# Keys spread from digits by TensorE, quartered loads, earlier zeroing and a stored one-hot in a four-layer graph network

## The chip, the cores and the metric

The kernel is one launch on one core of a Trainium2 chip. The metric is the device time of the launch in microseconds. Before the change it was 3574.64 us, the median of 3 runs (3573.5 to 3580.78 us). All times below are microseconds (us) unless marked ns.

## The reference

A graph of 3125 nodes with 32 features each and 100000 edges (`src`, `dst`, sorted by `dst`; `dst = int(3125 * u**2)`, so low numbers have many edges; `src` is uniform). Four layers, each `x = x + layer(relu(layernorm(x)))`:

```python
# layer 0: sum of edge attributes per source node, then a small network
agg = segment_sum(edge_attr_32, src); h = relu([x, agg] @ W1.T + b1)
out = batchnorm(h) @ W2.T + b2
# layer 1: a message per edge, summed per destination node
R = relu(w[:, None] @ w1 + b1) @ w2 + b2          # radial weights, 384 per edge
msg = tensor_product(R, directions(edge_attr_3), features[src])
out = zeros.at[dst].add(msg)                      # 32 values per edge
# layer 2: three rounds of out = clip(0.9 * A_w @ out + 0.1 * y, 0, 1), normalised weights
# layer 3: three rounds of z = batchnorm(relu(A_c @ z)), normalised counts and self-loops
```

`A_w` holds the summed weights and `A_c` the number of edges of each (source, destination) pair.

## The kernel before, in words

Nodes are padded to `NP` = 3200 (25 tiles of 128), edges to 100352, that is `CH` = 784 chunks of 128, one edge per partition. The host lays edge `784*p + c` at partition p of chunk c. A step is 4 chunks; there are `STEPS` = 196.

The matrices of layers 2 and 3 are built in DRAM in `both`, 3200 x 3200 pairs (count, weight), 82 MB. GpSimd first writes zeros there (41 DMAs, L543 and L547), and then adds one chunk after another with an indirect DMA that accumulates (`add`, L557): 128 rows of 8 bytes, at row `key = 3200*src + dst`. `add(c)` waits until `add(c-2)` has landed, so two are in flight. Edges of one chunk or of neighbouring chunks with the same key must be merged before: for that every key is compared with every other one of the group.

**First stage** (layer 0, and the merging of chunks 0 to 391): two steps make a group of 4 merged chunks. SyncE loads the group's 512 keys from `keys_dram`, broadcast to all 128 partitions (`load_keys`, L405, 256 KB), and per 4 steps 16 chunks of edge attributes (`load_attr`, L417, 256 KB). ScalarE squares the differences of keys (`compare_group`, L614) and turns them into a 0/1 matrix (L619). VectorE masks it (L1201), TensorE counts with small matmuls (L850 to L864), VectorE writes the entries and their places (L1209 to L1214). Besides, each step sums 4 chunks of attributes by source node: one-hots of the low part of the node number (ScalarE L639, L644; VectorE L1264) as weights, and as moving data the attributes times a one-hot of the high part (`prod0`, L1273, from the stored one-hot `high0` made at L1182), in 20 matmuls (`scatter0`, L879). All buffers are double.

**Between the stages** the small network of layer 0 runs, and the node table is written to `feat_dram` (L436). The constant tiles that all engines wait for (`s_const`) are made by GpSimd ahead of the zeroing.

**Second stage** (layer 1, and the merging of chunks 392 to 783): per step GpSimd gathers 4 chunks of node rows (`gather`, L565) and issues 2 adds, in program order after all adds of the first stage; TensorE does the merging matmuls, 8 matmuls for the radial weights of the next step (L949) and 20 for the sum by destination (`scatter`, L888); VectorE makes the messages (L1384 to L1422) and four products (`products`, L1242), each the message times the test `iota_a == a_dst` of the high part, computed on the spot. Chunk k of `scatter` waits for product k alone.

**Third stage**: layers 2 and 3 read `both` (L1472 on), 50 loads and then matrix products. It starts when all adds have landed.

Of the kernel before, what the change touches and what calls it, by code (L numbers as in the profile page):

```python
# [31 lines left out]
STEPS = CH // 4  # L32
PAIRS = CH // 2
# [52 lines left out]
def gnn_program(nc, x_in, src_in, dst_in, srcT_in, dstT_in, ea3_in, ea32_in, ew_in, ewT_in,  # L86
                w1T_in, b1_in, gamma_in, beta_in, w2T_in, b2_in, l1w1_in, l1b1_in, l1w2_in, l1b2_in,
                gam3_in, bet3_in, out):
    with ExitStack() as ctx:
# [9 lines left out]
        keys_dram = nc.dram_tensor("keys_dram", [CH, P], F32, kind="Internal").ap()  # L99
        feat_dram = nc.dram_tensor("feat_dram", [NP, ROW], F32, kind="Internal").ap()  # L100
# [20 lines left out]
        zc = sb("zc", [P, FEAT * 3], BF16)  # L121

# [37 lines left out]
        keyrow = edge(2, 4 * P)  # L160
# [64 lines left out]
        onehot0 = placed_at("onehot0", [P, 2, 4, PARTS * P], big_end - 4 * NP)  # L225
        zeros = big[:, 0, :]
# [10 lines left out]
        onehot = rings[:, 4 * 640:12 * 640].rearrange("p (q k n) -> p q k n", q=2, k=4)  # L237
        tmp_i = big[:, 3, 0:CH].bitcast(I32)
# [29 lines left out]
        s_rlen = sem("rel_len_ready")  # L268
        s_krow = [sem(f"keyrow{q}") for q in range(2)]
# [116 lines left out]
        def _(sp):  # L386
# [13 lines left out]
            sp.wait_ge(s_keysd, 16)  # L400

            def load_keys(first_c, n, q):

                row = keys_dram[ds(first_c, n), :].rearrange("(o c) p -> o (c p)", o=1)
                sp.dma_start(keyrow[:, q, 0:n * P], row.broadcast_to([P, n * P])).then_inc(s_krow[q], 16)  # L405
# [7 lines left out]
            def load_attr(u):  # L413

                if not first(u, 1):
                    sp.wait_ge(s_rows, u)
                sp.dma_start(attr[:, :, :].rearrange("p k f -> p (k f)"),  # L417
                             ea32_in[:, ds(u * (16 * FEAT), 16 * FEAT)]).then_inc(s_attr, 16)
# [19 lines left out]
            def load1(s, q, t):  # L438
                sp.wait_ge(s_gap, 6 * GROUPS0 + 2 * (s - 1) if not first(s) else 6 * (GROUPS0 - 1 + s))
                load_keys(2 * (s + STEPS), 2, q)  # L440
# [9 lines left out]
            for q in range(2):  # L450
                sp.wait_ge(s_add[q], 16 * PAIRS)
# [61 lines left out]
        def _(pool):  # L513
            pool.memset(zeros, 0.0).then_inc(s_zero, 1)
            pool.memset(ident[:, :], 0.0).then_inc(s_const, 1)
            pool.memset(earlier[:, :], 1.0).then_inc(s_const, 1)
            pool.memset(valid[:, :], 1.0).then_inc(s_const, 1)
            pool.wait_ge(s_const, 3)
            pool.affine_select(out=ident[:, :], in_=ident[:, :], compare_op=ALU.not_equal, fill=1.0,
                               base=0, pattern=[[-1, P]], channel_multiplier=1).then_inc(s_const, 1)  # L520

            pool.affine_select(out=earlier[:, :], in_=earlier[:, :], compare_op=ALU.is_gt, fill=0.0,
                               base=0, pattern=[[1, P]], channel_multiplier=-1).then_inc(s_const, 1)

            pool.affine_select(out=valid[:, :], in_=valid[:, :], compare_op=ALU.is_gt, fill=0.0,
                               base=NODES, pattern=[[-P, NA]], channel_multiplier=-1).then_inc(s_const, 1)
# [43 lines left out]
            for c in range(CH // 2):  # L570
# [245 lines left out]
        def _(pe):  # L816
# [79 lines left out]
            def phase0(s, k4, u):  # L896
# [5 lines left out]
                elif not is_last(s):  # L902
                    merge_open(g, slot)
# [700 lines left out]
```

## Time and profile before

| | before |
|---|---|
| median of 3 runs | 3574.64 us |
| the profiled execution's own time | 3583.88 us |
| its span | 3582.1 us |
| busy: TensorE / VectorE / ScalarE / GpSimd | 2928.3 / 2801.5 / 2302.2 / 2110.6 us |
| mean granted TensorE clock | 0.93 of full speed |
| bytes moved by DMA | 422.78 MB |

The profile is one execution, and its times are counted from the start of the span. Busy time leaves waits out. A releaser is what ended an idle time. In what follows, a period is the length of a stretch divided by the number of instructions of one group that it holds.

### The profile page before, as it was taken

What the parts mean: (1) busy time and instruction counts of PE and PEld (TensorE: products, weight loads), DVE (VectorE), ACT (ScalarE), POOL (GpSimd) and SP (SyncE); (2) the same over time, 40 slices, a digit from 0 to 9 for tenths busy, and PEclk for the clock granted to TensorE, in tenths of its full rate; (3) what the DMA queues carried; (4) which work ended last, traced back from release to release, by engine and by line L of the source; (5) the groups of instructions that cost most, each with busy time, mean ns of one, the idle gap of its engine ahead of it and who ended that gap; (6) DMA issues with size and microseconds to landing.
All of it is one profiled execution on the core that took longest, in us unless ns stands there. A gap on an engine that the chain in (4) does not pass through costs nothing. (4 is left out here: it accounts for less than half of the span.)

```text
span 3582.1 us, 70126 instructions
## 1 busy us (share of the span) xinstructions
PE 2928.3 (82%) x19604; PEld 2347.2 (66%) x19605; DVE 2801.5 (78%) x6559; ACT 2302.2 (64%) x3192; POOL 2110.6 (59%) x1633
## 2 busy tenths in 40 slices
PE   5877888888304999999999999999999976557656
PEld 4876787787203888888888888888888851113256
DVE  8879888888204999999999999999999983341054
ACT  6876888888203888888888888888888842230000
POOL 4017777777777777777777777777777740000000
PEclk9998999999556999999999999999999988788878
DMA  9973333333322222222222322232223259998830
GB/s 388 422 285 35 45 47 44 50 44 36 28 1 25 51 52 49 50 51 51 51 49 51 51 52 49 50 50 51 51 49 50 51 169 427 426 416 350 361 157 5
DMA packets 258165, 422.78 MB, mean 118 GB/s; under 512 B 149095, under 2 KB 174312, under 8 KB 251576
## 3 DMA queue, kind: packets, MB, share of 16 engines
q0 software_dynamic: 149536, 124.64, 19.9%
q1 hardware_dynamic: 92152, 224.49, 18.0%
q10 hardware_dynamic: 16416, 72.92, 5.0%
q8 instruction: 28, 0.46, 0.1%
q14 instruction: 33, 0.27, 0.0%
HBM read 290.44 MB, written 131.45 MB: 118 GB/s over the span
## 5 line engine op out<-in xcount | busy, mean ns | idle before, releaser
L557 POOL DMA_INDIRECT both<-kept x784 | 1279.0, 1631 | 547.1 <-issue 235.8
L888 PEld LDWEIGHTS ps<-prod,big 128*128 128x128 f32 x7840 | 1135.3, 190 | 179.5 <-DVE prod L1242 174.5
L888 PE MATMUL ps<-prod,big 128*128 128x170 f32 x7840 | 1185.3, 311 | 60.1 <-DVE prod L1242 60.0
L565 POOL DMA_INDIRECT kept<-feat_dram,kept x784 | 786.8, 1004 | 262.8 <-issue 178.3
L639 ACT ACTIVATE big<-iota_b,kept 128x640 f32<-128x640 f32 x1029 | 779.2, 815 | 13.6
L879 PE MATMUL ps<-prod,onehot 128*128 128x320 f32 x3920 | 671.6, 321 | 101.5 <-DVE prod L1273 76.7
L879 PEld LDWEIGHTS ps<-prod,onehot 128*128 128x128 f32 x3920 | 586.1, 190 | 117.7 <-DVE prod L1273 100.5
L644 ACT ACTIVATE big<-big 128x2560 f32<-128x2560 f32 x196 | 458.0, 2337 | 317.8 <-PE ps L888 317.7
L949 PE MATMUL ps<-w2mix,kept 65*128 65x384 f32 x1568 | 559.3, 500 | 21.7 <-ACT kept L691 20.4
L1413 DVE TENSOR_REDUCE kept<-kept 128x80 f32<-128x1280 f32 x392 | 561.2, 1470 | 0.0
L949 PEld LDWEIGHTS ps<-w2mix,kept 65*128 65x128 f32 x1568 | 284.1, 191 | 179.7 <-issue 25.5
L1403 DVE TENSOR_TENSOR kept<-ps,kept 128x384 f32<-128x384 f32 x784 | 394.8, 543 | 0.0
L587 POOL DMA_INDIRECT prod<-both,row_idx x8 | 7.7, 959 | 540.3 <-DVE row_idx L1519 526.5
L1273 DVE TENSOR_TENSOR prod<-kept 128x1280 fp32r<-128x1280 f32 x196 | 291.8, 1489 | 4.2
L1242 DVE SCALAR_TENSOR_TENSOR prod<-iota_a,kept 128x170 f32<-128x170 f32 x784 | 257.6, 391 | 46.9 <-DVE kept L1422 46.7
L1264 DVE TENSOR_SCALAR onehot<-iota_b,kept 128x640 fp32r<-128x640 f32 x539 | 289.6, 590 | 0.0
L1090 PE MATMUL ps<-big,zring 128*32 128x512 f32 (+3 forms) x400 | 184.8, 618 | 121.8 <-DMA big<-both 110.4
L1399 DVE TENSOR_TENSOR kept<-ps,kept 128x512 f32<-128x512 f32 x392 | 265.5, 677 | 0.0
L614 ACT ACTIVATE kept<-kept 128x128 f32<-128x128 f32 (+2 forms) x588 | 244.3, 494 | 11.7 <-DMA kept<-keys_dram 11.7
L631 ACT ACTIVATE kept<-kept 128x512 bf16<-128x512 f32 x196 | 123.5, 630 | 171.6 <-PE ps L834 157.5
L644 ACT ACTIVATE onehot<-big 128x640 fp32r<-128x640 f32 x196 | 171.3, 874 | 79.9 <-PE ps L879 71.1
L1472 DVE TENSOR_REDUCE row_max<-big 128x1 f32<-128x1600 f32 x50 | 91.0, 1819 | 164.0 <-DMA adj_c<-kept 107.1
(220 smaller groups left out, 2789.2 us busy)
## 6 DMA issues: line engine op xcount, KB each, us to landing
both<-big POOLq DMA_DIRECT2D x40, 2000.0 KB, 104.8
big<-both SPq DMA_DIRECT2D x50, 1600.0 KB, 10.6
adj_w<-kept ACTq DMA_DIRECT2D x32, 800.0 KB, 32.9
big<-adj_w SPq DMA_DIRECT2D x32, 800.0 KB, 12.4
big<-adj_w ACTq DMA_DIRECT2D x32, 800.0 KB, 11.8
kept<-keys_dram SPq DMA_DIRECT2D x98, 256.0 KB, 3.5
kept<-keys_dram SPq DMA_DIRECT2D x196, 128.0 KB, 2.9
kept<-in_wT SPq DMA_DIRECT2D x196, 128.0 KB, 2.8
```

The lines of the kernel that those rows point to most:

```text
L557: pool.indirect_dma_start(both, bass.IndirectOffsetOnAxis(ap=sc_idx[:, c:c + 1], axis=0), sc_val[:, c // 2, c % 2, :], None, compute_op=AL ...
L565: pool.indirect_dma_start(gath[:, s % 2, k, :], None, feat_dram, bass.IndirectOffsetOnAxis(ap=src_i[:, 4 * s + k:4 * s + k + 1], axis=0)). ...
L639: act.activation(dist[:, k, :], iota_b[:, :], ACT.Square, scale=-1.0, bias=bcol[:, ds(4 * s + k, 1)]).then_inc(s_dist[n], 4 // len(ks))
L644: act.activation(to[:, q, 0:len(ks), :], dist[:, 0:len(ks), :], ACT.Relu, scale=-1.0, bias=1.0).then_inc(s_oh[n], 1)
L879: mm = pe.matmul(ps[:, SUM0[part], 0:HI * 2 * FEAT], onehot0[:, q, k, part * P:(part + 1) * P], prod0[:, q, k, :, :].rearrange("p a m -> p ...
L888: mm = pe.matmul(part_sums(part, MSG), onehot[:, q, k, part * P:(part + 1) * P], prod[:, q, k, 0:HI * MSG], start=False, stop=False, skip_ ...
L949: mm = pe.matmul(ps[:, 4 + k, 0:384], hidT[:, q, k * P:(k + 1) * P], w2mix[:, :], start=True, stop=True)
L1264: ins = V.tensor_scalar(onehot0[:, q, k, :], iota_b[:, :], b_src[:, ds(4 * s + k, 1)], None, ALU.is_equal)
L1273: V.tensor_tensor(prod0[:, q, :, :, :], high0[:, ds(4 * s, 4), :].unsqueeze(3) .broadcast_to([P, 4, HI, 2 * FEAT]), rows0[:, 4 * k4:4 * k4 ...
L1399: V.tensor_tensor(T[:, :, 0:256].rearrange("p k (o x) -> p k o x", o=16), ps[:, 4 + 2 * g:6 + 2 * g, 0:256].rearrange("p k (o x) -> p k o ...
L1403: ins = V.tensor_tensor(T[:, k, 256:640].rearrange("p (u i x) -> p u i x", u=8, i=3), ps[:, 4 + 2 * g + k, 256:384].rearrange("p (u x) -> ...
L1413: V.tensor_reduce(res[:, q, 2 * g:2 * g + 2, 0:40], terms[:, g, :, :].rearrange("p k (o x) -> p k o x", x=16), AX, ALU.add).then_inc(s_red, 1)
```

## The change

Six edits, of which the last is on the host:

1. **Keys by TensorE (first stage).** VectorE cuts each key into three 8-bit digits (bf16), which are stored to a new DRAM tensor `parts_dram` of 3 rows. Per group SyncE loads [3, 512] of it (3 KB) in place of the 256 KB broadcast, and a matmul with the weights `places` (65536, 256, 1 in three rows) spreads the keys to all partitions in PSUM bank 7, from which ScalarE reads. The keys of the second stage still come by broadcast.
2. **Quartered loads.** The attributes of 4 steps come in four loads of 64 KB, issued one step after another; VectorE still waits for all four at the first of the 4 steps.
3. **Zeroing first.** GpSimd clears 2400 columns of the zero tile in place of 3200, starts the zeroing DMAs without waiting for the index loads, and makes the constant tiles after the fourth of them.
4. **No padding chunks.** Of the 784 chunks of the second half the last two (padding alone) are neither gathered nor added.
5. **Products by a stored one-hot.** Between the stages VectorE makes `high1` (bf16, 128x3920). In the second stage one `tensor_tensor` over 4 x 5 x 34 elements replaces the four products, and every chunk of `scatter` waits for all of it.
6. **Layout.** Chunk c now holds the 128 consecutive edges `128*c + p`.

```diff
-            sp.wait_ge(s_keysd, 16)
+            for t in range(3):
+                sp.dma_start(parts_dram[t:t + 1, :].rearrange("o (q j) -> (o q) j", q=112), digit[:, t, :]).then_inc(s_keysd, 16)
+            sp.wait_ge(s_keysd, 64)
             def load_group(g, slot):
                 if not first(g):
-                    sp.wait_ge(s_gap, 6 * (g - 1))
-                load_keys(4 * g, 4, slot)
+                    sp.wait_ge(s_rowps, g - 1)
+                sp.dma_start(keyp[:, slot, :], parts_dram[:, ds(g * (4 * P), 4 * P)]).then_inc(s_keyp[slot], 16)
+            def load_attr(s, k4):
+                sp.dma_start(attr[:, 4 * k4:4 * k4 + 4, :].rearrange("p k f -> p (k f)"),
+                             ea32_in[:, ds(s * (4 * FEAT), 4 * FEAT)]).then_inc(s_attr, 16)
             def load0(u):
-                load_group(u * 2, 0)
-                load_attr(u)
-                load_group(u * 2 + 1, 1)
+                for k4 in range(4):
+                    if k4 % 2 == 0:
+                        load_group(u * 2 + k4 // 2, k4 // 2)
+                    if not first(u, 1):
+                        if k4 == 0:
+                            sp.wait_ge(s_rows, u)
+                        else:
+                            sp.wait_ge(s_prod[0], u * 16 + (4 * k4 - 16))
+                    load_attr(u * 4 + k4, k4)
...
-            pool.memset(zeros, 0.0).then_inc(s_zero, 1)
+            pool.memset(zeros[:, 0:NA * ROW], 0.0).then_inc(s_zero, 1)
             pool.wait_ge(s_zero, 1)
-            pool.wait_ge(s_in["idxT"], 32)
-            pool.wait_ge(s_in["idx"], 32)
-            pool.wait_ge(s_in["w"], 16)
...
+                if t == 3:
+                    setup_tiles()
...
-                    gather(s + 1, range(4))
+                    gather(s + 1, range(min(4, USED - 4 * (s + 1))))
...
-                    act.activation(key_gap[:, lo * P:(lo + n) * P], keyrow[:, slot, col * P:(col + n) * P], ACT.Square,
+                    act.activation(key_gap[:, lo * P:(lo + n) * P], ps[:, 7, col * P:(col + n) * P], ACT.Square,
                                    scale=-1.0, bias=of).then_inc(s_gap, 1)
...
+            def spread_keys(g, slot):
+                pe.wait_ge(s_keyp[slot], 8 * (g - slot) + 16)
+                if not first(g, 1):
+                    pe.wait_ge(s_gap, 6 * g)
+                pe.matmul(ps[:, 7, :], places[:, :], keyp[:, slot, :], start=True, stop=True).then_inc(s_rowps, 1)
...
-                pe.wait_ge(s_prod[1], 4 * s + k + 1)
+                pe.wait_ge(s_prod[1], 4 * s + 4)
...
+            link(V.scalar_tensor_tensor(out=keyT_i, in0=srcT, scalar=float(NP), in1=dstT, op0=ALU.mult, op1=ALU.add))
+            V.tensor_scalar(digit_i[:, 0, :], keyT_i, 16, None, ALU.arith_shift_right)
+            V.tensor_scalar(digit_i[:, 1, :], keyT_i, 8, 255, ALU.arith_shift_right, ALU.bitwise_and)
+            link(V.tensor_scalar(digit_i[:, 2, :], keyT_i, 255, None, ALU.bitwise_and))
+            V.tensor_copy(digit, digit_i).then_inc(s_keyT, 1)
...
-                    dve.wait_ge(s_sum[1], 4 * s - 8 + k + 1)
-                V.scalar_tensor_tensor(
-                    out=prod[:, q, k, 0:HI * MSG].rearrange("p (a m) -> p a m", a=HI),
-                    in0=iota_a[:, :].unsqueeze(2).broadcast_to([P, HI, MSG]),
-                    scalar=a_dst[:, ds(4 * s + k, 1)], in1=res[:, q, k, 8:42].unsqueeze(1).broadcast_to([P, HI, MSG]),
-                    op0=ALU.is_equal, op1=ALU.mult).then_inc(s_prod[1], 1)
+                    dve.wait_ge(s_sum[1], 4 * s - 4)
+                V.tensor_tensor(prod[:, q, :, 0:HI * MSG].rearrange("p k (a m) -> p k a m", a=HI),
+                                high1[:, ds(4 * s, 4), :].unsqueeze(3).broadcast_to([P, 4, HI, MSG]),
+                                res[:, q, :, 8:42].unsqueeze(2).broadcast_to([P, 4, HI, MSG]),
+                                ALU.mult).then_inc(s_prod[1], 4)
...
+        return a.reshape((CH, P) + a.shape[1:]).swapaxes(0, 1).reshape(P, -1)
```

## Rows read from the trace of the kernel before

**Rows 1.** The page's 40 equal slices of the span, busy share in tenths.
```profile
PE   5877888888304999999999999999999976557656
DVE  8879888888204999999999999999999983341054
POOL 4017777777777777777777777777777740000000
DMA  9973333333322222222222322232223259998830
```

**Rows 2.** Waits over the whole span: in total, times, longest.
```profile
POOL both L557 <- DMA both<-big: 201.7, 1, 201.7
...
DVE kept L1384 <- DMA kept<-feat_dram,kept: 180.5, 1, 180.5
```

**Rows 3.** Order of time, GpSimd: start, length, line, tiles, idle before.
```profile
9.39 1.01 POOL L543 DMA_DIRECT2D both<-big  x1 [3.48 <-DMA kept<-in_w]
...
243.26 1.72 POOL L557 DMA_INDIRECT both<-kept  x1 [201.72 <-DMA both<-big]
```

**Rows 4.** Order of time, all engines, around both ends of the second stage's late start.
```profile
940.16 0.38 SPq L436 DMA_DIRECT2D feat_dram<-big  x1
...
1114.27 1.03 POOL L565 DMA_INDIRECT kept<-feat_dram,kept  x1 [0.30 <-issue]
...
1120.66 0.28 DVE L1384 TENSOR_TENSOR kept<-kept 128x96 f32<-128x96 f32 x1 [180.53 <-DMA kept<-feat_dram,kept]
```

**Rows 5.** Groups of instructions, GpSimd, 400 to 890 us (first stage).
```profile
L557 POOL DMA_INDIRECT both<-kept x212 | 357.6, 1687 | 133.7 <-DMA both<-kept 73.5 <-issue 60.2
```

**Rows 6.** The same, 950 to 1110 us (other engines idle).
```profile
L557 POOL DMA_INDIRECT both<-kept x83 | 127.8, 1540 | 33.3 <-issue 28.1 <-DMA both<-kept 5.2
```

**Rows 7.** DMA queues and issues, 60 to 220 us (zeroing): MB, share; KB, us to landing.
```profile
q0 software_dynamic: 7970, 59.98, 89.3%
q1 hardware_dynamic: 4153, 7.55, 12.4%
...
kept<-keys_dram SPq DMA_DIRECT2D x19, 256.0 KB, 10.7
kept<-in_ea SPq DMA_DIRECT2D x10, 256.0 KB, 8.2
```

**Rows 8.** Stretches: busy PE, PEld, DVE, ACT, POOL; clock, DMA share, GB/s.
```profile
10.00:12.00 2.00, 0.00 (x0) 0.00 (x0) 1.90 (x4) 0.00 (x0) 2.00 (x4) 1.00 0.15 25
...
230.00:244.00 14.00, 12.38 (x97) 11.20 (x96) 12.10 (x30) 10.35 (x15) 0.74 (x1) 1.00 0.32 76
```

**Rows 9.** Order of time, VectorE and ScalarE at the start.
```profile
6.63 1.09 DVE L1173 SCALAR_TENSOR_TENSOR prod<-prod 112x896 f32<-112x896 int32 x1
...
10.91 0.63 DVE L1152 CAST kept<-big 128x784 f32<-128x784 int32 x1
...
25.94 1.28 ACT L614 ACT_TABLE_LOAD   x1 [25.94 <-DVE kept L1193]
```

**Rows 10.** Groups, 400 to 890 us: the first stage's products.
```profile
L1273 DVE TENSOR_TENSOR prod<-kept 128x1280 fp32r<-128x1280 f32 x115 | 171.2, 1489 | 2.6
```

**Rows 11.** Groups, whole span.
```profile
L1182 DVE TENSOR_TENSOR kept<-iota_a,kept 128x3920 f32<-128x3920 f32 x1 | 4.2, 4242 | 0.0
...
L820 PE MATMUL ps<-zero_bf 128*128 128x512 bf16 x6 | 2.7, 587 | 1.4 <-DVE zero_bf L1159 1.3 <-issue 0.2
```

**Rows 12.** Groups, 1500 to 2500 us (second stage).
```profile
L565 POOL DMA_INDIRECT kept<-feat_dram,kept x438 | 440.0, 1005 | 144.5 <-issue 99.4 <-DVE kept L1403 41.6 <-DMA both<-kept 3.5
L557 POOL DMA_INDIRECT both<-kept x218 | 349.4, 1603 | 66.4 <-issue 66.4
...
L1399 DVE TENSOR_TENSOR kept<-ps,kept 128x512 f32<-128x512 f32 x218 | 147.6, 677 | 0.0
L1242 DVE SCALAR_TENSOR_TENSOR prod<-iota_a,kept 128x170 f32<-128x170 f32 x436 | 143.3, 391 | 26.5 <-DVE kept L1422 26.5
```

**Rows 13.** Order of time, one step of the second stage.
```profile
2007.24 6.04 PE L888 MATMUL ps<-prod,big 128*128 128x170 f32 x40 [0.37 <-DVE prod L1242]
...
2013.27 2.83 PE L949 MATMUL ps<-w2mix,kept 65*128 65x384 f32 x8
...
2014.90 0.16 DVE L1228 TENSOR_REDUCE kept<-ps 128x12 f32 x1
...
2016.33 2.86 PE L888 MATMUL ps<-prod,big 128*128 128x170 f32 x18 [0.23 <-DVE prod L1242]
```

More of the change, by code:

```diff
@@ L32 @@
 STEPS = CH // 4
+USED = -(-EDGES // P)
 PAIRS = CH // 2
@@ L159, in gnn_program @@
         near = edge(2, GROUPS0)
-        keyrow = edge(2, 4 * P)
+        keyrow = edge(2, 2 * P)
+        keyp = edge(2, 4 * P, dt=BF16, parts=3)
         key_gap = edge(12 * P)
@@ L225, in gnn_program @@
         onehot0 = placed_at("onehot0", [P, 2, 4, PARTS * P], big_end - 4 * NP)
+        high1_at = kept_end - CH * HI * 2
+        high1 = nc.alloc_sbuf_tensor_at("high1", [P, CH, HI], BF16, offset=high1_at)
         zeros = big[:, 0, :]
@@ L268, in gnn_program @@
         s_rlen = sem("rel_len_ready")
+        s_keyp = [sem(f"key_parts{q}") for q in range(2)]
+        s_rowps = sem("group_keys_in_psum")
         s_krow = [sem(f"keyrow{q}") for q in range(2)]
@@ L438, in load1 @@
             def load1(s, q, t):
-                sp.wait_ge(s_gap, 6 * GROUPS0 + 2 * (s - 1) if not first(s) else 6 * (GROUPS0 - 1 + s))
-                load_keys(2 * (s + STEPS), 2, q)
+                if not first(s):
+                    sp.wait_ge(s_gap, 6 * GROUPS0 + 2 * (s - 1))
+                load_keys(s + STEPS, q)
                 if not first(s):
@@ L522, in _ @@
[L522 to L526, printed above, removed]
-            pool.iota(iota_b[:, :], [[1, PARTS * P]], base=0, channel_multiplier=0,
-                      allow_small_or_imprecise_dtypes=True).then_inc(s_const, 1)
@@ L575, in _ @@
                 if s + 1 < STEPS:
-                    gather(s + 1, range(4))
+                    gather(s + 1, range(min(4, USED - 4 * (s + 1))))
                 if s >= BEHIND:
-                    for c in range(2):
-                        add(2 * (STEPS + s - BEHIND) + c)
+                    for c in range(2 * (STEPS + s - BEHIND), min(2 * (STEPS + s - BEHIND) + 2, USED)):
+                        add(c)
             eighths = both[0:BIG, :].rearrange("(s d) o -> s (d o)", d=EIGHTH)
@@ L903, in phase0 @@
                     merge_open(g, slot)
+                if k4 % 2 and not is_last(s, 4):
+                    spread_keys(g + 1, 1 - slot)
                 scatter0(s, k4, 2)
@@ L1322, in _ @@
             dve.wait_ge(s_sum[0], CH)
+            V.tensor_tensor(high1[:, :, :], iota_a[:, :].unsqueeze(1).broadcast_to([P, CH, HI]),
+                            a_dst.unsqueeze(2).broadcast_to([P, CH, HI]), ALU.is_equal)
             V.memset(res[:, :, :, 41:42], 1.0)
@@ L1425, in phase1 @@
                 dve.wait_ge(s_wcol, s + 1)
-                for k in range(4):
-                    products(s, q, k)
+                products(s, q)
             steps(dve, phase1)
@@ L1579, in padded, with chunks @@
         return _np.concatenate([a, _np.full((rows - a.shape[0],) + a.shape[1:], fill, a.dtype)])
-    src, dst = (padded(i[k], CH * P, NP - 1).reshape(P, CH) for k in ("src", "dst"))
-    w = padded(i["edge_weight"], CH * P, 0).reshape(P, CH)
+    def chunks(name, fill):
+        a = padded(i[name], CH * P, fill)
+        return a.reshape((CH, P) + a.shape[1:]).swapaxes(0, 1).reshape(P, -1)
+    src, dst = (chunks(k, NP - 1) for k in ("src", "dst"))
+    w = chunks("edge_weight", 0)
     data = {
```

81 lines of the change are left out of this document (48 added, 33 removed).

## The prediction

> **What bounds the kernel now.** I read the slices first [rows 1]. TensorE and VectorE are 80 to 90% busy up to slice 10, and again at 9 from slice 14 to 31. Between these lie two slices in which only GpSimd works. At the front, GpSimd has two almost empty slices while DMA is full. The waits tell the same in microseconds [rows 2]: GpSimd waits 201.7 us for the zeroing, and VectorE 180.5 us for the first gathered rows. So there are three stretches with different limits.
>
> *First stage.* It is GpSimd's queue that ends it. The first add starts at 243.26 [rows 3]. The node table goes to DRAM at 940.16, so from about 947 on the second stage could start. But the gathers stand behind all 392 adds, and the first is issued at 1114.27 [rows 4]. Thus 871 us for 392 adds, a period of 2.22 us, and VectorE follows 6.4 us later, at 1120.66. Whatever VectorE, ScalarE and TensorE gain before 947 brings nothing; what counts is when zeroing ends and the add's period.
>
> The period has parts. In 400 to 890 us it is 490/212 = 2.31 us: 1.69 busy, 0.35 waiting for an earlier add to land, 0.28 issue [rows 5]. In 950 to 1110 us, with nothing beside it, it is 160/83 = 1.93: 1.54, 0.06 and 0.34 [rows 6].
>
> *Second stage.* 218 adds, two per step, are 109 steps in 1000 us: 9.17 us a step [rows 12]. In one step the scatter begins at 2007.24, the next after it at 2016.33. In between TensorE has finished its last radial matmul at 2016.10, 8.86 us after it began, and waits 0.23 us for the first product [rows 13]. VectorE has no idle time in its big groups; its only wait is 26.5 us for its own message [rows 12]. So VectorE sets 9.17, TensorE's floor is 8.86, and GpSimd's is (440.0 + 349.4 + 99.4 + 66.4 + 3.5)/109 = 8.80 [rows 12]. Three engines within 4%.
>
> *Third stage.* Nothing of the change is in it.
>
> **The change part by part.**
>
> *Zeroing.* GpSimd's first zeroing DMA leaves at 9.39, when the loads have landed [rows 3]. After it DMA goes from nearly idle (share 0.15 in 10 to 12 us [rows 8]) to full. Starting first regains only this gap: I count 2.4 us (0.85 x 2 plus 0.7 just before), since the loads' bytes must be moved anyway. During zeroing all 16 DMA engines are full. SyncE's queue takes 12.4% of 160 us, 19.8 us, for 29 loads of equal size, 19 of them keys [rows 7]: 13.0 us per 160, 8.1%. Over 222 us that is 18 us that vanish (the 3 KB loads are taken as nothing). The quartered attributes move the same bytes. If a quarter costs in proportion nothing changes; if each costs like a whole load it is 6.8 us x 3 per 160 us, +28 us. Proportion is nearer, as the bytes are what fills the engines: I take +3. At the end one straggler stays: DMA is only 0.32 busy from 230 to 244 [rows 8] while GpSimd still waits. I leave it. Zeroing ends at 243.3 - 2.4 - 18 + 3 = 226; bounds 218 and 251.
>
> The Trainium skill, DMA: Bandwidth & Descriptors, Latency and other measured facts, says that DMA engines 7 and 15 are usually slower than the others; the trace shows such a tail without naming the engine, and by that rule too it stays.
>
> *The adds' period.* The 0.35 us of waiting comes from other transfers in the engines' way. Two thirds of the stage's loads by number and size were key broadcasts (98 against 49). Taking them away leaves 0.12. Busy time goes from 1.69 to that of the second stage, 1.60 [rows 12], where VectorE is as busy and loads are smaller. Issue stays at 0.28 to 0.33. Sum 2.0. Bounds: 1.93, nothing beside it, and 2.22, nothing gained. It can't go below what VectorE delivers, 4 entries per group of 8.3 us (2.08 each), but there is a stock of some 85 chunks when zeroing ends, and it isn't used up at 2.0 before the stage ends. Adds end at 226 + 392 x 2.0 = 1010.
>
> The Trainium skill, DMA: Bandwidth & Descriptors, Bandwidth, holds that transfers under 64 KB are dominated by their descriptors and that larger batches are better. By it the quartering would lose what the keys give back, and the period would stay near 2.2; the row has the 256 KB loads hindering the adds, and I go by the row.
>
> *Is the second stage ready by then?* Before: 947. VectorE at the start: one more pass like L1173 (1.09), three shifts of 896 (0.7 each, from 0.63 for 784 [rows 9]) and a conversion of 2688 (2.2), then four tiny ones: +6.5 us, all ahead of the 25.94 at which ScalarE starts. The four digit stores and the first loads now meet full queues: +5. Per group a matmul of 512 bf16 columns: between 0, hidden in TensorE's waits, and its 0.59 [rows 11]; I take 0.15, x98 = +15. A quarter of attributes is issued one step (4.2 us) and about 1 us ahead of its use, but landed 8.2 us after issue in zeroing [rows 7]: VectorE stalls about 2.6 us in each 4 steps, x11 = +29. After zeroing it lands in time. `high1` is as large as `high0`, 4.24 us [rows 11]: +4. One stall of 12 us around 250, where keys were queued behind `x` and `rel`, is roughly halved: -7. Total 1000, against 1010. So GpSimd still ends it, by 10 us; I add 2 us for the closeness. VectorE starts the second stage at 1018 where it was 1120.66: **-102 us**. ScalarE reading PSUM in place of SBUF is put at nothing; it would have to cost 10 us in all before it shows.
>
> *Second stage.* The four products take 143.3/109 = 1.31 us a step. One tensor_tensor of 680 elements lies between 512 (677 ns [rows 12]) and 1280 (1489 ns [rows 10]): 677 + 168 x 1.057 = 855 ns. VectorE's step falls by 0.46 to 8.71, below TensorE's 8.86 and GpSimd's 8.80. The new wait: the first scatter chunk starts after the whole product instead of after the first of four, 0.46 us later. Behind it on TensorE stand the merging and radial matmuls of the next step. This wait shows only while VectorE is the late one; once TensorE is, products lie ready. Does VectorE in turn wait for TensorE? The merge is done at about 2013.2 and used at 2014.90 [rows 13], 1.7 us of slack; the double buffer needs the scatter two steps back. Both hold. What is late next is TensorE, with GpSimd 0.06 behind. I take 8.89: 196 x 0.28 = **-55 us**. Bounds: 0 (the wait and the saving cancel) and 8.80 (-73).
>
> *No padding.* Two adds and two gathers at the very end, behind which nothing waits once TensorE is last: 0, at most 6 us.
>
> *Layout.* A chunk's 128 edges now have nearly one destination, so its rows lie at multiples of 25600 bytes apart, source times pitch, instead of all over the matrix. The number of adds and of bytes is the same. Nothing in the trace prices this; the adds' landing must stay within the two periods that the double issue gives. I put it at 0 and keep it as a rival.
>
> *Sum.* 3583.9 (the profiled execution) - 102 - 55 = 3427. That execution was 9.2 us above the median of the runs; as the runs themselves spread from 3573.5 to 3580.8, I give the median: **3418 us**.
>
> **The rivals.**
>
> *A: adds keep their pace.* The hindrance comes from VectorE or the attributes, not from the keys. For it: busy time rises to 1.69 whenever VectorE works. Against it: in the second stage it is 1.60 with VectorE fuller. Period 2.22: adds end at 226 + 870 = 1096, start at 1102, -18; with -55, less 9: 3502.
>
> *B: nothing from the products.* Whole-product waiting, or a slower product with its bf16 input, keeps 9.17. The product would have to take 1.31 us. Time 3583.9 - 102 - 9 = 3473.
>
> *C: the first stage's engines end last.* Spreading costs its full 0.59 a group (+43) and the quarters stall outside zeroing as well. Ready at about 1050, VectorE starts there: 3583.9 - 71 - 55 - 9 = 3449.
>
> *D, the slower side: same-destination adds land late.* 128 accumulations on addresses at one pitch collide in DRAM. Each pair of adds would then wait. With one wait of 2.2 us per pair, of the size seen between pairs now and then, the period is 1.9 + 1.1 = 3.0: start at 226 + 1176 + 6 = 1408, +287, less 55, less 9: 3807. It decides from a period of 2.41 on: 226 + 392p + 6 = 1120.7 + 55. Against it: the pitch is multiplied by random sources, and 0.06 us of waiting in the quiet stretch says there is room.
>
> The Trainium skill, DMA: Bandwidth & Descriptors, Latency and other measured facts, reports halved rates for HBM rows at pitches of large powers of two; 25600 bytes is none, and no run here shows that pattern.
>
> **How the numbers follow.** Forecast 61% (its own range 3385 to 3455), A 11%, B 12%, C 7%, D 9%. Low end: period 1.93 with everything ready at 983 (start 989, -132) and a step of 8.80 (-73) give 3370. High end: A, 3502. Of 100, some 5 lie below and 10 to 12 above. A difference under 0.2% (7 us) can't be told from no change here. Faster by more: 0.90; within: 0.02; slower: 0.08, D less what of it stays under the point.
>
> **What would show it.** The first add between 218 and 235; L557 at a period of 2.0 in 400 to 890 with its wait for landed adds below 0.15 us each; the first gather within 15 us of 1012, with all of VectorE's work before it done. In the second stage L1242's successor at 0.86 us, steps of 8.9, TensorE's wait for products gone. In zeroing, VectorE waiting for attributes once in four steps. The prediction is wrong if the adds still wait for each other, if gathers are issued and VectorE isn't there yet, or if a step stays at 9.1 or more.

## The result, and the profile after

The changed kernel takes 3484.49 us (median of 4 runs, 3480.62 to 3487.19), the kernel before beside it 3576.33 us (4 runs, 3573.5 to 3580.78). The ratio is 0.9741, with a 95% interval of 0.9724 to 0.9758: 2.6% faster. The forecast was 3418 us in a range of 3370 to 3502. The range and the sign held; the gain was 92 us where 157 were forecast. The profiled execution took 3486.41 us with a span of 3484.7, against 3583.9 and 3582.1 before: 97 us less.

The slices of the page, after (each digit is a busy share in tenths, the clock line the granted share of full speed):

```profile
PE   3788788888877999999999999999999976657656
DVE  6678888888877999999999999999999973450064
POOL 4037888888866777777777777777777720000000
PEclk9999799899988999999999999999999987798878
DMA  9953222222213333333333333333333369999830
```

Against [rows 1]: after zeroing the DMA line stands at 2 in slices 5 to 11, where it stood at 3, since the key broadcasts are gone (the page has 12 to 16 GB/s in slices 5 to 10, and 36 to 50 before). The two slices in which GpSimd worked alone are gone too: the first stage's engines now work a slice longer, and the adds end a slice earlier. VectorE stands at 6, 6 and 7 in the first three slices, where it stood at 8, 8 and 7; in the rest of the first stage the tenths hardly tell the two kernels apart.

The waits over the whole span (in total, times, longest):

```profile
POOL both L577 <- DMA both<-big: 181.1, 1, 181.1
ACT kept L635 <- PE ps L865: 151.2, 96, 12.7
...
POOL kept L585 <- DMA feat_dram<-big: 35.1, 1, 35.1
...
DVE kept L1301 <- DMA kept<-in_ea: 29.5, 9, 5.1
```

L577, the add, answers to L557 in [rows 2]. The second row is new: ScalarE waits 151 us for the spreading matmuls at L865. The third is new as well: GpSimd, its adds done, waits 35 us for the node table. The last is VectorE waiting for quartered attributes. The order of time says where:

```profile
222.06 1.90 POOL L577 DMA_INDIRECT both<-kept  x1 [181.14 <-DMA both<-big]
...
1021.88 1.54 POOL L577 DMA_INDIRECT both<-kept  x1 [0.30 <-issue]
...
1051.95 0.38 SPq L454 DMA_DIRECT2D feat_dram<-big  x1
1058.52 1.02 POOL L585 DMA_INDIRECT kept<-feat_dram,kept  x1 [35.10 <-DMA feat_dram<-big]
...
1065.50 0.26 DVE L1426 TENSOR_TENSOR kept<-kept 128x96 f32<-128x96 f32 x1 [13.58 <-DMA kept<-feat_dram,kept]
```

Zeroing ends 21.2 us earlier than in [rows 3] (forecast 17). The last add starts at 1021.88 and takes 1.54 us, so GpSimd would be free for gathers from 1023.4 on. But the table leaves only at 1051.95, 112 us later than in [rows 4], so VectorE starts the second stage at 1065.50 in place of 1120.66: -55 us, where -102 was forecast. The groups of 400 to 890 us (busy, mean ns, idle before):

```profile
L577 POOL DMA_INDIRECT both<-kept x243 | 407.8, 1678 | 84.3 <-issue 84.3
L907 PE MATMUL ps<-prod,onehot 128*128 128x320 f32 x2072 | 377.6, 338 | 66.3 <-ACT onehot L665 64.7
...
L1313 DVE TENSOR_TENSOR prod<-kept 128x1280 fp32r<-128x1280 f32 x104 | 155.2, 1492 | 0.9
...
L635 ACT ACTIVATE kept<-ps,kept 128x128 f32<-128x128 f32 (+2 forms) x312 | 119.4, 482 | 80.5 <-PE ps L865 80.5
...
L865 PE MATMUL ps<-kept,places 3*128 3x512 bf16 x52 | 22.6, 435 | 0.4
```

The adds' waits for one another, 73.5 us in [rows 5], are gone and 243 adds fit where 212 did: a period of 490/243 = 2.02. But 104 products fit where 115 did [rows 10]: a step takes 4.71 us, it took 4.26. The second stage, 1500 to 2500 us:

```profile
L916 PE MATMUL ps<-prod,big 128*128 128x170 f32 x4469 | 674.3, 310 | 12.6 <-DVE prod L1283 9.2
...
L585 POOL DMA_INDIRECT kept<-feat_dram,kept x446 | 432.6, 970 | 135.9 <-issue 134.4 <-DMA both<-kept 1.5
...
L1283 DVE TENSOR_TENSOR prod<-high,kept 128x680 f32<-128x680 f32 x112 | 97.3, 869 | 25.3 <-DVE kept L1464 25.3
```

There 112 steps fit where 109 did [rows 12]: 8.93 us a step, 9.17 before, 8.89 forecast. The product takes 869 ns against a forecast of 855. TensorE is now busy in 987.4 of the 1000 us (967.1 before), and over the whole span its matmuls at L916 wait 16.7 us for products where they waited 60.0: it is close to its limit, as forecast. The third stage's loads are issued at 2824.00, before at 2920.59: 96.6 of the 97 us are made by then, 55 at the start and the rest in this stage.

### The profile page after: what moved, and what is told of

It is laid out like the page before. It is cut to its first block and busy times, and to the rows that moved or that the text cites. A ratio compares the mean times of both kernels' runs of the same rounds, so it can differ in the third digit from the quotient of the medians.

```text
span 3484.7 us, 69264 instructions
## 1 busy us (share of the span) xinstructions
PE 2978.0 (85%) x19702; PEld 2385.9 (68%) x19703; DVE 2742.2 (79%) x5981; ACT 2291.3 (66%) x3192; POOL 2104.3 (60%) x1629
## 5 line engine op out<-in xcount | busy, mean ns | idle before, releaser
L577 POOL DMA_INDIRECT both<-kept x782 | 1295.9, 1657 | 443.4 <-issue 205.1
L916 PEld LDWEIGHTS ps<-prod,big 128*128 128x128 f32 x7840 | 1134.3, 190 | 136.8 <-DVE prod L1283 133.2
L916 PE MATMUL ps<-prod,big 128*128 128x170 f32 x7840 | 1183.2, 310 | 22.2 <-DVE prod L1283 16.7
L585 POOL DMA_INDIRECT kept<-feat_dram,kept x782 | 760.8, 973 | 279.8 <-issue 232.2
L907 PE MATMUL ps<-prod,onehot 128*128 128x320 f32 x3920 | 719.4, 339 | 133.5 <-ACT onehot L665 116.2
L907 PEld LDWEIGHTS ps<-prod,onehot 128*128 128x128 f32 x3920 | 639.6, 207 | 167.9 <-issue 121.1
L635 ACT ACTIVATE kept<-ps,kept 128x128 f32<-128x128 f32 (+2 forms) x588 | 225.0, 482 | 151.2 <-PE ps L865 151.2
L1313 DVE TENSOR_TENSOR prod<-kept 128x1280 fp32r<-128x1280 f32 x196 | 292.3, 1491 | 1.9
L1122 PEld LDWEIGHTS ps<-big,zring 128*32 128x32 f32 x400 | 45.4, 125 | 261.0 <-issue 249.2
L757 ACT ACTIVATE kept<-big 128x1600 f32<-128x1600 f32 x50 | 82.2, 1648 | 192.3 <-issue 76.3
L1283 DVE TENSOR_TENSOR prod<-high,kept 128x680 f32<-128x680 f32 (+1 forms) x196 | 170.3, 869 | 43.8 <-DVE kept L1464 43.4
```

The source lines that it names most:

```text
L577: pool.indirect_dma_start(both, bass.IndirectOffsetOnAxis(ap=sc_idx[:, c:c + 1], axis=0), sc_val[:, c // 2, c % 2, :], None, compute_op=AL ...
L585: pool.indirect_dma_start(gath[:, s % 2, k, :], None, feat_dram, bass.IndirectOffsetOnAxis(ap=src_i[:, 4 * s + k:4 * s + k + 1], axis=0)). ...
L907: mm = pe.matmul(ps[:, SUM0[part], 0:HI * 2 * FEAT], onehot0[:, q, k, part * P:(part + 1) * P], prod0[:, q, k, :, :].rearrange("p a m -> p ...
L916: mm = pe.matmul(part_sums(part, MSG), onehot[:, q, k, part * P:(part + 1) * P], prod[:, q, k, 0:HI * MSG], start=False, stop=False, skip_ ...
L1313: V.tensor_tensor(prod0[:, q, :, :, :], high0[:, ds(4 * s, 4), :].unsqueeze(3) .broadcast_to([P, 4, HI, 2 * FEAT]), rows0[:, 4 * k4:4 * k4 ...
```

## The experiments

Each diff is against the changed kernel, but for `d1`, which is against the kernel before. The kernel before took 3567.01 us on the chip of the first group (`e1`, `e2`, `e4`, `e5`), 3585.52 on that of the second (`d1`, `e6` to `e8`) and 3585.82 on that of the third (`c0`, `e9`, `f6`, `f7`), so ratios are compared, or rows. Even ratios of different groups are not alike to better than 0.4%: the changed kernel itself stood at 0.9741 and, in the third group, at 0.9705. Where less than that is at stake, the rows decide.

### Is the wait for the spreading a loop?

In the trace of after, in order of time:

```profile
606.14 1.49 DVE L1313 TENSOR_TENSOR prod<-kept 128x1280 fp32r<-128x1280 f32 x1
...
606.50 2.30 ACT L635 ACTIVATE kept<-ps,kept 128x128 f32<-128x128 f32 x6 [0.97 <-PE ps L865]
...
611.84 1.27 ACT L665 ACTIVATE onehot<-big 128x1280 fp32r<-128x1280 f32 x1
613.24 1.97 PE L907 MATMUL ps<-prod,onehot 128*128 128x320 f32 x10 [2.07 <-ACT onehot L665]
...
615.49 0.60 PE L865 MATMUL ps<-kept,places 3*128 3x512 bf16 x1
...
616.31 2.04 ACT L635 ACTIVATE kept<-ps,kept 128x128 f32<-128x128 f32 x5 [1.36 <-PE ps L865]
```

ScalarE's squares (606.50) need the spread. Its one-hots (611.84) stand behind them on its queue. The scatter (613.24) needs the one-hots and waits 2.07 us. The next group's spread (615.49) stands behind that scatter on TensorE. This turn is 616.31 - 606.50 = 9.8 us, for two steps (in the mean of 400 to 890 they take 9.4); before, two steps took 8.5.

`e1_spread_early`: the spread is put ahead of the step's scatters.

```
             def phase0(s, k4, u):
+                if k4 % 2 and not is_last(s, 4):
+                    spread_keys(g + 1, 1 - slot)
                 scatter0(s, k4, 0)
...
-                if k4 % 2 and not is_last(s, 4):
-                    spread_keys(g + 1, 1 - slot)
```

> The changed kernel with one move: TensorE issues the spreading matmul of the next group at the head of its odd step, ahead of the scatter that waits for ScalarE's one-hots, not after the merging matmuls. Theory L (a loop: the spread stands behind matmuls that wait for ScalarE, and ScalarE waits for the spread): ScalarE's wait for L865, 151 us in the changed kernel, falls below 20; the first stage's step in 400 to 890 us falls from 4.6 to about 4.25 us; the node table is stored at about 1000 instead of 1052, GpSimd's adds (end 1024) then end last, and the time is about 3484 - 28 = 3456. Rival P (the matmul's own time on a full TensorE, the lower clock, or ScalarE reading PSUM): the step stays at 4.55 or more, the wait moves elsewhere, and the time stays within 10 us of 3484.

Measured: ratio 0.9771 (0.9748 to 0.9793). The table leaves at 988.33, 63.6 us earlier. The 96 waits at L865 are gone (one of 36.0 at the start stays), 116 products fit in 400 to 890, a step of 4.22, and the clock is 1.00 where it was 0.91. So the loop is shown, with its size: 63 us. The time does not follow, though: 3486.6 us where 3456 was expected. The adds, with no wait at all, have become slower:

```profile
L577 POOL DMA_INDIRECT both<-kept x231 | 414.7, 1795 | 76.2 <-issue 76.2
```

1795 ns against 1678. The last add is issued at 1050.62, the first gather right behind it at 1052.46. What one side gave, the other took: a faster VectorE hinders GpSimd's adds. Why?

### What makes an add slow?

`d1_vector_in_quiet`: the kernel before, in whose quiet stretch GpSimd adds alone, gets three series of VectorE instructions there. They only cost time, the arithmetic is unchanged.

```
+            for _ in range(45):
+                link(V.tensor_tensor(sq[:, :, :], cen[:, :, :], cen[:, :, :], ALU.mult))
+            for _ in range(45):
+                link(V.tensor_reduce(st[:, 0, :], cen[:, :, :], AX, ALU.add))
+            for _ in range(70):
+                link(V.tensor_scalar(sq[:, :, :], cen[:, :, :], 1.0, None, ALU.mult))
```

> The kernel before, in whose quiet stretch (950 to 1110 us, GpSimd's adds alone at 1.54 us each) VectorE now runs three series on its own tiles, results unused: 45 products of two SBUF tensors (0.99 us each), 45 reductions of one SBUF tensor (0.99 us each), 70 scalings of one SBUF tensor (0.58 us each). Theory V (a VectorE instruction that reads two SBUF tensors holds up an add that starts beside it, which is why adds take 1.68 to 1.85 us in the first stage and why they slow down when VectorE speeds up): adds beside the products take 1.9 us or more in the mean, beside the reductions 1.54. The scalings, too, may hold adds up, by the end of theirs. Rival W (adds are slowed by transfers, by TensorE or ScalarE, or by the load on the queue): all three series leave the adds at 1.54 to 1.57 us.

Measured: 3580.03 us (one run, so its time tells nothing fine), and the groups of four windows: 970 to 987 beside products with two SBUF inputs, 990 to 1030 beside reductions, 1035 to 1075 beside scalings, 1085 to 1110 alone. In the first three hardly any other transfer runs (0 to 1 GB/s); in the last, 5 GB/s, the first gathers begin at its end.

```profile
L1379 DVE TENSOR_TENSOR both_tmp<-both_tmp 128x800 f32<-128x800 f32 x18 | 17.9, 993 | 0.6
L557 POOL DMA_INDIRECT both<-kept x9 | 15.6, 1736 | 3.9 <-issue 2.4 <-DMA both<-kept 1.4
```
```profile
L1381 DVE TENSOR_REDUCE st<-both_tmp 128x25 f32<-128x800 f32 x40 | 39.5, 988 | 1.4
L557 POOL DMA_INDIRECT both<-kept x22 | 33.9, 1539 | 8.8 <-issue 7.1 <-DMA both<-kept 1.7
```
```profile
L1383 DVE TENSOR_SCALAR both_tmp<-both_tmp 128x800 f32<-128x800 f32 x64 | 38.7, 605 | 2.2
L557 POOL DMA_INDIRECT both<-kept x21 | 33.5, 1594 | 7.4 <-issue 7.4
```
```profile
L557 POOL DMA_INDIRECT both<-kept x11 | 17.0, 1542 | 3.6 <-issue 3.6
```

The order of time shows the edge: the products end and the reductions begin at 987.93, between these two adds.

```profile
984.48 1.75 POOL L557 DMA_INDIRECT both<-kept  x1 [0.30 <-issue]
986.53 1.75 POOL L557 DMA_INDIRECT both<-kept  x1 [0.30 <-issue]
988.59 1.54 POOL L557 DMA_INDIRECT both<-kept  x1 [0.30 <-issue]
```

VectorE is as busy with reductions as with products, and beside reductions an add takes 1539 ns, as it does alone. Beside products it takes 1736, mostly 1750. So it is the kind of VectorE instruction, not its busy share or the DMA traffic. I had expected 1.9 or more; over 945 to 985, where 128 KB loads run in part, it is 1792. The Trainium skill, SBUF — State Buffer, Who interferes with whom, states that a VectorE instruction with two SBUF inputs contends with a GpSimd instruction that reads SBUF, and that `tensor_reduce` never contends on trn2. The rows agree with both: 1736 and 1539 ns.

The first stage's big product (L1313) is such an instruction, 1.49 us long. `e6_product_halves` and `e7_product_quarters` are `e1` with that product in 2 and in 4 pieces (shown for 4; the halves have `range(0, 4, 2)` and 2 chunks each):

```
-                V.tensor_tensor(prod0[:, q, :, :, :], high0[:, ds(4 * s, 4), :]
...
+                for k in range(0, 4, 1):
+                    V.tensor_tensor(prod0[:, q, k:k + 1, :, :], high0[:, ds(4 * s + k, 1), :]
...
```

> The kernel with the early spread (e1), and the first stage's product of 1280 elements (1.49 us) cut in two instructions of 640 (about 0.8 us each). Theory V: an add is held up for at most half as long, so the mean add falls from 1.80 to about 1.68 us and the period in 400 to 890 us from 2.12 to about 2.02; adds end near 1015 instead of 1052; the step grows by 0.1 us (table stored near 1005); the second stage starts near 1025 instead of 1059 and the time is about 3486 - 30 = 3456. Rival W: the mean add stays at 1.80, the time within 8 us of e1's.

> As e6, but in four instructions of 320 elements (about 0.47 us each). Theory V: the mean add falls further, to about 1.62 us; but VectorE has 0.4 us more per step, so the table is stored near 1050 and the first stage's engines end last: time about 3475. Rival W: mean add 1.80 unless the slower step alone lowers it, as in the changed kernel (1.68 at a step of 4.6 us).

Measured: 3462.57 us, ratio 0.9651 (0.9632 to 0.9671), and 3456.75 us, 0.9635 (0.9618 to 0.9652). For 400 to 890, first the halves, then the quarters:

```profile
L577 POOL DMA_INDIRECT both<-kept x240 | 407.4, 1698 | 84.4 <-issue 76.3 <-DVE kept L1255 4.9 <-DMA both<-kept 3.2
...
L1314 DVE TENSOR_TENSOR prod<-kept 128x640 fp32r<-128x640 f32 x228 | 178.0, 822 | 2.6
```
```profile
L577 POOL DMA_INDIRECT both<-kept x243 | 403.5, 1661 | 88.5 <-issue 80.8 <-DMA both<-kept 4.9 <-DVE kept L1255 2.8
...
L1314 DVE TENSOR_TENSOR prod<-kept 128x320 fp32r<-128x320 f32 x433 | 183.6, 486 | 2.5
```

The halves keep nearly the pace of `e1` (228/2 = 114 steps where it had 116) and VectorE spends more time in them (178.0 us, 172.9 there), yet the adds go from 1795 to 1698 ns. So it is not the time that products take in all, but the length of one. With quarters the step is also slower (433/4 = 108), so their 1661 ns owe a part to the pace.

The order of time shows that an add is held until the product in its way ends. Two adds of `e1`, each with the product that was running when it started:

```profile
355.40 1.49 DVE L1313 TENSOR_TENSOR prod<-kept 128x1280 fp32r<-128x1280 f32 x1
355.65 2.66 POOL L577 DMA_INDIRECT both<-kept  x1 [0.30 <-issue]
...
334.75 1.48 DVE L1313 TENSOR_TENSOR prod<-kept 128x1280 fp32r<-128x1280 f32 x1
335.62 2.03 POOL L577 DMA_INDIRECT both<-kept  x1 [0.30 <-issue]
```

The products end at 356.89 and 336.23, the adds at 358.31 and 337.65, both 1.42 us later. Between 300 and 880 us this holds for every add whose product began at least 0.05 us before it and ran on for at least 0.4: 57 adds in `e1` and 37 in the changed kernel, which end 1.41 to 1.43 us after the product. Adds that start 0.05 to 0.4 us ahead of a product take 1.55 us in the mean, about as alone.

The adds of the halves ended at 1031.56, not near 1015 as expected, and the quarters' table left 26 us before the expected 1050. In the quarters' kernel the last add is issued at 1020.25, the table leaves at 1024.17, and GpSimd waits only 8.96 us before its first gather at 1030.75; VectorE starts at 1037.7, 28 us before the changed kernel.

### What the other parts of the change are worth

`e2_keys_broadcast`: the keys come by 256 KB broadcasts again, the rest stays.

```
+        keyrow = edge(2, 4 * P)
...
+                load_keys(4 * g, 4, slot)
...
-                pe.matmul(ps[:, 7, :], places[:, :], keyp[:, slot, :], start=True, stop=True).then_inc(s_rowps, 1)
```

> The changed kernel with its first edit undone whole: first-stage keys by 256 KB broadcast, no digits, no spread. The other edits stay. Theory K (the broadcasts were what held up the adds): adds in 400 to 890 us back at a period of 2.2 to 2.3 with waits for landed adds, zeroing ends 15 to 18 us later than in the changed kernel (222), adds end at about 1110, VectorE starts the second stage at about 1117 though the table is stored near 960, time about 3484 + 50 = 3535. Rival Q (it was the 256 KB attribute loads): the period stays near 2.05, adds end at about 1040, and the time falls to about 3460, since the first stage is then quick again.

Measured: 3574.09 us, ratio 1.002 (1.0007 to 1.0032). The first add starts at 231.68, the last at 1143.16, a period of 2.33. Worse than any theory had it: without digits none of the gain is left. The adds of 400 to 890 say why:

```profile
L573 POOL DMA_INDIRECT both<-kept x198 | 365.4, 1845 | 124.1 <-issue 50.4 <-DMA both<-kept 43.8 <-DVE kept L1231 29.9
```

They wait for landings again, they wait for VectorE, and each takes longer. The keys' share of zeroing is 231.68 - 222.06 = 9.6 us, where I had put 18. The second stage keeps its gain (VectorE 1151.4 to 2892.9, 1741.5 us), and the adds use it up. So the digits are worth 1.002 - 0.9741 = 2.8%, about 100 us; by the traces, VectorE starts the second stage 86 us later without them (1151.4 against 1065.5). Why these adds are slower than the 1687 ns of [rows 5], at the same pace of products (114 against 115), can be seen in part: between 300 and 880 us, 66 of 237 adds find the product running 0.2 to 0.4 us after their start, where 20 of 251 did before. Why they meet it so much oftener stays open.

`e4_four_products`: the second stage's products as before.

```
-                V.tensor_tensor(prod[:, q, :, 0:HI * MSG].rearrange("p k (a m) -> p k a m", a=HI),
...
+                V.scalar_tensor_tensor(
...
+                    op0=ALU.is_equal, op1=ALU.mult).then_inc(s_prod[1], 1)
```

> The changed kernel with the four computed products and the wait per chunk back. Theory: the second stage's step goes from 8.93 back to 9.17 us, 196 x 0.24 = 47 us, less 4 us for the missing stored one-hot: about 3528. Rival (GpSimd's queue or the clock made the step shorter, not the products): step stays at 8.95, time near 3481.

Measured: 3518.68 us (one run), a step of 1000/109 = 9.17. VectorE's second stage lasts 1055.9 to 2843.0, 1787.1 us against 1743.3 in the changed kernel (1065.5 to 2808.8): in that stage the product by one stored one-hot is worth 43.8 us, as this theory had it. Making `high1` takes 4.24 us ahead of it.

`e5_old_layout`: edges laid out, and chunks padded, as before.

```
-USED = -(-EDGES // P)
+USED = CH
...
-        return a.reshape((CH, P) + a.shape[1:]).swapaxes(0, 1).reshape(P, -1)
+        return a.reshape(P, -1)
```

> The changed kernel with the edges laid out as before (edge 784*p + c), and therefore all 784 chunks gathered and added. Theory (layout costs nothing): adds in 400 to 890 us at the same 2.02 us without waits for landed adds, the same second-stage step, and a time within 8 us of 3484. Rival D (same-destination adds land late or early): the adds' period or their waits differ by more than 0.05 us.

Measured: 3491.68 us (one run, whose time is too coarse to tell). The adds take 1676 ns with 2.3 us of waiting in 400 to 890, where the changed kernel's take 1678; over the stage the period is 2.033 against 2.045 (last add at 1015.89), and VectorE's second stage lasts 1744.0 against 1743.3. Nothing of rival D's collisions shows.

`e8_zero_after_loads`: the zeroing DMAs wait for the input loads, as before.

```
+            setup_tiles()
+            pool.wait_ge(s_in["idxT"], 32)
+            pool.wait_ge(s_in["idx"], 32)
+            pool.wait_ge(s_in["w"], 16)
...
-                if t == 3:
-                    setup_tiles()
```

> The changed kernel with the constant tiles made first and the zeroing DMAs waiting for the five index loads, as before. Theory (my term of 2.4 us): zeroing ends at 225 to 229 instead of 222, and the first product comes 3 to 10 us earlier than at 50.3, since the digit stores meet emptier queues; the table (which decides in the changed kernel) is stored 3 to 8 us earlier, time about 3479. Rival (issuing first is worth its 6 us in full): zeroing ends at 228 or later, the first product does not move.

Measured: 3488.61 us (one run). First add 225.59, so issuing the zeroing first is worth 3.5 us (2.4 put). The first product is at 50.7, not earlier: the late start is not due to the zeroing's place. Two other runs split it: the first product is at 40.6 without the digits' round (`e2`) and at 43.9 with whole loads (`e9`, below), against 50.3. That expectation was wrong.

### Whole loads, and the changed kernel once more

`c0_changed_again` is the changed kernel, to stand beside the others of its group.

> The changed kernel itself, once more beside the next three, so that they are compared on one chip: about 0.974 of the kernel before, table stored at about 1052, adds ending at about 1024.

Measured: 3481.81 us, ratio 0.9705 (0.9686 to 0.9724), a little below the 0.974 expected; the rows repeat (table 1050.35, last add 1022.24), and VectorE starts at 1064.3.

`e9_whole_loads` is `e1` with attributes in 256 KB loads:

```
-                for k4 in range(4):
...
+                load_group(u * 2, 0)
+                load_attr(u)
+                load_group(u * 2 + 1, 1)
...
-                    dve.wait_ge(s_attr, 64 * u + 64)
+                    dve.wait_ge(s_attr, 16 * u + 16)
```

> The kernel with the early spread (e1), with the second edit undone: 16 chunks of attributes in one 256 KB load, asked for as soon as the buffer is free. Theory (quartering costs the first stage and helps the adds): VectorE's wait for attributes during zeroing, 29.5 us in the changed kernel, is gone and the table is stored 20 to 30 us earlier than e1's 988, which decides nothing; adds wait again for landed adds once in 17 us, some 0.1 us each, so they end 20 to 40 us later than in e1 (1052), time about 3510. Rival (quartering gave the adds nothing, the keys did it all): adds' period and time as in e1, 3480 to 3490.

`f6_halves_whole_loads` and `f7_quarters_whole_loads` are `e6` and `e7` with the same edit.

> Product in halves (e6) with whole loads. By the theory of e9: slower than e6 by 20 to 40 us, about 3490. By its rival: the same as e6, near 3462, since adds end it there.

> Product in quarters (e7) with whole loads. By the theory of e9: the table comes 25 us earlier than e7's 1024 but the adds, which end at 1022 there, end 20 to 40 us later: 3470 to 3490. By its rival: adds end at about 1022 and the table is ready before, time about 3448, the best of all.

Measured, with the parent kernels for comparison:

```
                     time (95% of ratio)                 table    last add  VectorE   add, ns
c0 (the changed)     3481.81  0.9705 (0.9686, 0.9724)    1050.35  1022.24   1064.3    1646
e1                   3486.6   0.9771 (0.9748, 0.9793)     988.33  1050.62   1058.8    1795
e9 (e1, whole)       3491.09  0.9732 (0.9708, 0.9757)     944.82  1061.23   1069.5    1780
e6                   3462.57  0.9651 (0.9632, 0.9671)     996.95  1031.56   1039.9    1698
f6 (e6, whole)       3477.54  0.9697 (0.9674, 0.972)      955.99  1049.99   1058.2    1721
e7                   3456.75  0.9635 (0.9618, 0.9652)    1024.17  1020.25   1037.7    1661
f7 (e7, whole)       3467.3   0.9672 (0.9649, 0.9696)     981.23  1038.21   1046.4    1678
```

Table is when the node table leaves, the last column the mean add of 400 to 890. The times of `e9` and `e1` come from different groups and do not decide (by time `e9` is the slower, by ratio the faster); the rows do. Whole loads free the first stage's engines by 41 to 44 us, and the waits for attributes go. The adds end 11 to 18 us later, though. At least two things go into that: zeroing ends 5 us later (first adds at 226.0 to 226.3, 221 in the parents), and the adds wait more for landings, 6 to 11 us in 400 to 890 where the parents' wait 0 to 5. That VectorE is further ahead from the start may be a third; it was not tried alone. The adds end the stage in `e1`, in `e6` and in the three with whole loads; in `e7` GpSimd is done first and waits 9 us for the table. With whole loads VectorE starts the second stage 9 to 18 us later each time. So the quartering is worth its price here. The expectations had the table's gain too small (20 to 30 us) and the adds' loss too large (20 to 40), and the times fell between the theory's and its rival's.

The quarters with early spreading, `e7`, are the fastest. Beside kernels before of 3585.52 and 3585.82 us, they take 3456.75 where the changed kernel took 3481.81: 25 us less (the two were not run on one chip).

## Why the forecast was right in sign and too large

One reading was loose: TensorE's digits up to slice 10 are 5 to 8, not 8 and 9 [rows 1]; nothing hangs on it.

*First add 226: held* (222.06), by errors that cancel, which is luck. Keys' bytes were worth 9.6 us, not 18; quarters cost nothing and save 5 where I put +3; issuing first gave 3.5 for 2.4. These make 18 of the 21.2 us; the rest was not traced. A queue's share of 16 full engines overstated what its removal gives back.

*The adds' period 2.0: held* (2.045 over 392 adds, last one issued at 1021.88; with it the stage's adds end at 1023, forecast 1010). Its parts did not. Waiting went to 0, below the 0.12 put; busy stayed at 1.68, where I had taken the second stage's 1.60. That figure carries the holds by VectorE's instructions and is not one number: 1.54 alone, 1.74 beside products with two inputs. What VectorE can deliver was reckoned with 8.3 us a group; [rows 10] has 490/115 x 2 = 8.5, and the changed kernel took 9.4. The stock of merged chunks covered that: no add waited for VectorE in 400 to 890.

*"Is the second stage ready by then?" is the step that failed.* The sum made it 1000, 10 us ahead of the adds. It was 1058: table out at 1051.95, 6.6 us for landing. By the prediction's own sign, a first gather within 15 us of 1012 with VectorE's work done before it, this step was wrong: the gather came at 1058.52, and it waited for the table. From the first product to the table: 905.5 us before, 1001.7 after, 938.6 in `e1`. So:
- The spreading: put at 0.15 a group, +15, as TensorE time. The matmul is 0.44 us. What it costs is the order: a round of ScalarE and TensorE waiting for each other, 1001.7 - 938.6 = 63 us. This is the mis-sized term.
- Quarters stalling in zeroing: +29, measured 29.5 in 9 waits. Their whole price is more, 988.33 - 944.82 = 43.5 us (`e1` against `e9`), 6 of it before the first product.
- The start: +11.5, measured +15.6 (50.28 against 34.7), quarters included.
- The stall near 250, put at -7: not read by itself, but `e9`, with neither loop nor quarters, takes 900.9 us from first product to table, 4.6 less than before.
- ScalarE reading PSUM: nothing, held (482 ns a square, 494 before).

With the loop gone the forecast's order of events does come true: `e1` has the engines ready at 995. But the adds then end at 1052, not at 1010. So the sum would have failed there next: it treated the adds and VectorE as independent. VectorE's 63.6 us made the adds end 28.7 later (1050.62 against 1021.88). This coupling, not the loop, is why 102 was out of reach: `e7`, in which both are eased, starts at 1037.7, -83.

*Second stage: -55 forecast, -41 measured.* VectorE's stretch went from 1784.0 to 1743.3. Product and step were right within 0.04 us, but 0.04 over 196 steps is 8 us. The middle's rate, 0.24 a step, would make 47; the other 6 are lost outside 1500 to 2500 and were not traced further.

*Rivals.* A: its cause, VectorE's work, is real, its outcome (1096) is not, as the waiting was the keys'. B, whose 3473 lies nearest the measured time, is refuted by `e4`: the nearness is chance. C has the right end, engines ready at 1050, by another way: the matmul itself takes 0.44 us and not 0.59, it is the order that costs 63, and after zeroing the quarters do not stall (116 and 115 products in 400 to 890, `e1` and `e9`). D is refuted by `e5`.

*The range.* Its high end, 3502, came from rival A, adds that keep a period of 2.22. The period fell as forecast, and what made the time 66 us longer than 3418 was none of A's. That the range held owes more to its width than to its reasons.

## What to carry to other kernels

An instruction added to an engine's queue is priced by what it waits for and what waits for it: follow its inputs' and outputs' engines round once, and if the path returns, the round's length is the step, whatever the busy shares say. Where a background engine works through a list beside the others, its time per item is not a constant; before counting on it, ask which of the neighbours' instructions hold it, and try shorter ones, even at more total time. A stage that ends by the later of two engines gives only the distance to the second, so read both ends before summing gains.

## What the hardware showed that was not expected

- GpSimd's adding DMA took 1736 ns beside back-to-back VectorE products with two SBUF inputs (993 ns each), 1594 beside scalings, 1539 beside reductions, 1542 alone. Cutting the first stage's 1490 ns product to 822 and 486 brought the mean add from 1795 to 1698 and 1661.
- An add that starts while such a product runs ends 1.41 to 1.43 us after the product does, however much of the product was left; one that starts 0.05 to 0.4 us ahead of it is not held (1.55 us).
- This is why the changed kernel's adds (1678, again 1646) beat those of `e1` (1795) by more than 104 products against 116 explain. In 300 to 880, adds that find L1313 running 0.2 to 0.4 us after their start are 47 of 286 in the changed kernel and take 2.06 us in the mean; in `e1` they are 65 of 274 and take 2.26. The others take 1.61 and 1.65. Over 1.54 us, the adds held by L1313 (those that end 1.41 us after it) spend 25 us in the changed kernel and 47 us in `e1`. That is 0.08 of the 0.11 us between the two means. Why the periods of the two engines fall on each other so, no run here varied alone.
- Where TensorE waits in the round, its granted clock averaged 0.91 (400 to 890); in `e1`, with the waits gone, 1.00. The stretches, with busy PE, PEld, DVE, ACT, POOL, then clock, DMA share and GB/s, for after and for `e1`:

```profile
400.00:890.00 490.00, 415.26 (x2955) 370.87 (x2954) 405.98 (x857) 382.20 (x593) 406.02 (x243) 0.91 0.26 15
```
```profile
400.00:890.00 490.00, 444.95 (x3292) 395.90 (x3292) 438.08 (x955) 421.44 (x660) 414.14 (x231) 1.00 0.25 16
```

So part of the loop's 63 us is slower matmuls: 338 ns a scatter matmul against 318 before. How much of the 63 that makes was not separated.
- The 256 KB key broadcasts cost the adds 0.29 us of period (2.33 against 2.045 over the stage), though in 400 to 890 they raise the DMA engines' share only from 0.26 to 0.33. Part of it is that the adds meet the product oftener (66 of 237, above).
